# Leaving out the drain ahead of most vector and scalar instructions of a fused transformer layer

## The reference

```python
mod = (silu(c) @ wmod)                       # six vectors: sa, ca, ga, sb, cb, gb
ga, gb = sign(.) * maximum(abs(.), 0.25)     # each of the two gates
h = layernorm(x) * (1 + ca) + sa
q, k, v = split(h @ w_qkv)                   # 8 heads of 128
q_phi, k_phi = elu(q @ proj) + 1, elu(k @ proj) + 1        # 64 features
s = q_phi . k_phi over a window of 7 positions             # banded
x = x + ga * (normalised(s @ v) @ w_out + b_out)
h = layernorm(x) * (1 + cb) + sb
xn, se = rms_norm(h), rms_norm(slot_embeds)                # 4096 slots
logits = xn @ se.T
slots = softmax over positions(logits).T @ xn
processed = gelu(slots @ w1) @ w2                          # hidden 4096
out = x + gb * (softmax over slots(logits) @ processed)
```

## Time and profile before

| what | value |
|---|---|
| median of three runs | 4747.43 us |
| the three runs | 4679.46, 4799.58, 4747.43 us |
| the profiled execution | 4651.43 us |
| its span on the slowest core, from the first to the last instruction | 4649.3 us |
| spans of the eight cores | 4616.8 to 4649.3 us |
| busy time of TensorE's matmuls | 2645.6 us (57%) |
| busy time of VectorE | 1050.6 us (23%) |
| busy time of ScalarE | 688.5 us (15%) |

### The profile page before, as it was taken

How to read it: one execution, slowest core, us unless ns; L and a number is a source line. 1 busy time by engine, 2 the same in 40 slices (tenths; PEclk the granted TensorE clock), 3 DMA queues, 4 the chain that set the end, 5 groups by cost and what they waited for, 6 DMA issues and landing times. The chain is left out here.

```text
span 4649.3 us, 35458 instructions; the slowest of 8 cores (4616.8 to 4649.3 us)
## 1 busy us (share of the span) xinstructions
PE 2645.6 (57%) x11776; PEld 1229.4 (26%) x11776; DVE 1050.6 (23%) x2012; ACT 688.5 (15%) x1181; POOL 547.1 (12%) x1021
## 2 busy tenths in 40 slices
PE   4245344344333555555555558888599974554454
PEld 0222112111111222222222223333144432332222
DVE  1533222222554222222222200000301011111111
ACT  0101111111111111111111112222000001111111
POOL 4000000000000111111111125445200000000000
PEclk5567555565666777777777779999699986666667
DMA  8120111111111111111111151111622321111111
GB/s 119 50 48 19 23 23 23 36 32 41 55 55 41 34 34 34 34 34 37 41 37 34 32 104 62 62 59 62 124 73 73 87 63 55 54 63 55 54 55 59
DMA packets 138961, 241.91 MB, mean 52 GB/s; under 512 B 34967, under 2 KB 80279, under 8 KB 137758
## 3 DMA queue, kind: packets, MB, share of 16 engines
q0 software_dynamic: 78864, 138.49, 13.1%
q1 hardware_dynamic: 59918, 101.16, 7.2%
HBM read 201.85 MB, written 83.89 MB: 61 GB/s over the span
## 5 line engine op out<-in xcount | busy, mean ns | idle before, releaser
L1066 PE MATMUL pH<-slots_fm,w_bf 128*128 128x512 bf16 x2048 | 486.6, 401 | 117.6 <-DMA h_sp<-hbuf 73.4
L1153 PE MATMUL pP<-w_bf,hblk 128*128 128x512 bf16 x2048 | 458.3, 386 | 35.7 <-DVE w_bf L1131 20.6
L922 PE MATMUL pL<-xn_fm,sefs 128*128 128x512 bf16 x1024 | 282.3, 444 | 52.3 <-DVE sefs L913 52.3
L95 POOL DMA_DIRECT2D h_sp<-hbuf x512 | 271.9, 539 | 331.6 <-ACT hbuf L1077 320.9
L1066 PEld LDWEIGHTS pH<-slots_fm,w_bf 128*128 128x128 bf16 x2048 | 205.6, 102 | 398.2 <-issue 188.6
L994 PE MATMUL pDs<-xn_tm,atm 128*128 128x512 bf16 x1024 | 274.8, 436 | 31.6 <-DVE atm L986 31.6
L1153 PEld LDWEIGHTS pP<-w_bf,hblk 128*128 128x128 bf16 x2048 | 199.5, 98 | 295.6 <-issue 61.8
L1274 PE MATMUL pO<-proc_sm,w_smb 128*128 128x512 bf16 x1024 | 257.3, 419 | 15.8 <-DVE w_smb L1263 15.8
L95 POOL DMA_DIRECT2D L_sp<-lch x256 | 136.3, 541 | 1044.1 <-ACT lch L953 1005.7
L946 ACT ACTIVATE ach<-pL,colA,rscale_all 128x512 bf16<-128x512 f32 x128 | 99.5, 778 | 964.7 <-DVE colA L935 956.2
L977 PE MATMUL pAt<-ident_bf_s,ach 128*128 128x128 bf16 x512 | 64.8, 306 | 295.3 <-ACT ach L946 263.4
(11 more groups left out here) (185 smaller groups left out, 2481.2 us busy)
## 6 DMA issues: line engine op xcount, KB each, us to landing
L_sp<-lch POOLq DMA_DIRECT2D x256, 128.0 KB, 2.2
h_sp<-hbuf POOLq DMA_DIRECT2D x512, 64.0 KB, 1.8
lblk<-L_sp SPq DMA_DIRECT2D x8, 4096.0 KB, 16.7
se_st<-slot_embeds POOLq DMA_DIRECT2D x32, 512.0 KB, 3.6
wsl<-wmod POOLq DMA_DIRECT2D x96, 128.0 KB, 7.9
xst<-x SPq DMA_DIRECT2D x16, 512.0 KB, 3.3
xrs<-x SPq DMA_DIRECT2D x16, 512.0 KB, 3.8
x_sp<-x2b POOLq DMA_DIRECT2D x16, 512.0 KB, 4.5
```

The costliest lines, as they stand in the source:

```text
L95: self.ops[eng].append(lambda e: e.dma_start(dst, src).then_inc(h, 16))
L922: lmk = P.run("tensor", lambda e, buf=buf, j=j, nb=nb: e.matmul(pL[nb][:, 0:512], se_fs[buf][:, j * 128:(j + 1) * 128], xn_fm[:, j * N + n ...
L1066: e.matmul(pH[pbase + q][:, 0:512], w1_bf[:, j * HID + hc * 128:j * HID + (hc + 1) * 128], slots_fm[:, j * S + hf * 2048 + q * 512: j * S ...
L1153: e.matmul(pP[2 * (st % 2) + half][:, 0:512], h_blk[blk % 2][:, hc * HBW + st * 128: hc * HBW + (st + 1) * 128], w2_bf[:, hc * D + half * ...
```

## The change

`run` gets an argument `chain`, and the drain is put out only where it is true. A second method, `runf`, calls `run` without it. The calls at which the instruction does not read what the instruction right before it on the same engine has written become `runf`; the others stay. Of VectorE's 2012 drains 471 are left, of ScalarE's 950 there are 70 left: 1541 and 880 are gone, 2421 in all. No instruction is added, taken away or moved on any engine, and every semaphore wait stays where it was. The whole of the mechanism, and some of the 44 places at which it is used (the others are of the same form):

```diff
-    def run(self, eng, fn, sem=None, k=1):
-        if eng in ("vector", "scalar"):
+    def run(self, eng, fn, sem=None, k=1, chain=True):
+        if chain and eng in ("vector", "scalar"):
             self.ops[eng].append(lambda e: e.drain())
...
+    def runf(self, eng, fn, sem=None, k=1):
+        return self.run(eng, fn, sem, k, chain=False)
...
-                P.run("vector", lambda e, xs=xs, c=c: e.reduce_sum(
+                P.runf("vector", lambda e, xs=xs, c=c: e.reduce_sum(
                     colC[:, c:c + 1], xs[:], AX.X))
                 P.run("vector", lambda e, c=c: e.tensor_scalar(
                     colC[:, c:c + 1], colC[:, c:c + 1], 1.0 / D, None, ALU.mult))
...
                 for j in range(DJ):
-                    lastev = P.run("vector", lambda e, pt=pt, j=j, i=i: e.tensor_scalar(
+                    lastev = P.runf("vector", lambda e, pt=pt, j=j, i=i: e.tensor_scalar(
                         h1p[:, j * NP + 3 + i * 128: j * NP + 3 + i * 128 + 128],
...
                 for nb in range(4):
-                    P.run("vector", lambda e, nb=nb: e.reduce_max(
+                    P.runf("vector", lambda e, nb=nb: e.reduce_max(
                         colA[:, 8 + nb:9 + nb], pL[nb][:, 0:512], AX.X))
                 P.run("vector", lambda e: e.reduce_max(
                     colA[:, 12:13], colA[:, 8:12], AX.X))
...
-                    sfm_last = P.run("vector", lambda e, jj=jj, sc=sc: e.tensor_copy(
+                    sfm_last = P.runf("vector", lambda e, jj=jj, sc=sc: e.tensor_copy(
                         slots_fm[:, jj * S + sc * 128:jj * S + sc * 128 + 128],
...
                     for q in range(4):
-                        gel = P.run("scalar", lambda e, q=q, hc=hc, pbase=pbase:
-                                    e.activation(
+                        gel = P.runf("scalar", lambda e, q=q, hc=hc, pbase=pbase:
+                                     e.activation(
...
                 w2f_mk.append(P.run("vector", lambda e, hc=hc: e.tensor_tensor(
                     w2_bf[:, hc * D:(hc + 1) * D], w2_bf[:, hc * D:(hc + 1) * D],
-                    gb_rep[:], ALU.mult), "v"))
+                    gb_rep[:], ALU.mult), "v", chain=(hc == 0)))
```

More of the change, by code:

```diff
@@ L455, in build @@
                                 P.wait("vector", "v", m_vz)
-                            vev.append(P.run("vector",
-                                             lambda e, pv=pv, i=i, half=half, r=rows:
-                                             e.tensor_copy(
+                            vev.append(P.runf("vector",
+                                              lambda e, pv=pv, i=i, half=half, r=rows:
+                                              e.tensor_copy(
                                 v_tm[0:r, i * D + half * 512:i * D + half * 512 + 512],
@@ L535, in build @@
                         for b4 in (2 * h2, 2 * h2 + 1):
-                            P.run("vector", lambda e, b4=b4: e.tensor_scalar(
+                            P.runf("vector", lambda e, b4=b4: e.tensor_scalar(
                                 t_min_q[:, (b4 % 2) * 512:(b4 % 2) * 512 + 512],
                                 pp[4 + b4 % 2][0:64, 0:512], 0.0, None, ALU.min))
-                            P.run("vector", lambda e, b4=b4: e.tensor_scalar(
+                            P.runf("vector", lambda e, b4=b4: e.tensor_scalar(
                                 t_min_k[:, (b4 % 2) * 512:(b4 % 2) * 512 + 512],
                                 pp[b4 % 2][0:64, 0:512], 0.0, None, ALU.min))
-                        m_tmin = P.run("vector", lambda e: e.memset(colD[:, 1:2], 0.0), "v")
+                        m_tmin = P.runf("vector", lambda e: e.memset(colD[:, 1:2], 0.0), "v")
                         P.wait("scalar", "v", m_tmin)
-                        P.run("scalar", lambda e: e.activation(
+                        P.runf("scalar", lambda e: e.activation(
                             t_min_q[:], t_min_q[:], AF.Exp))
-                        m_exp = P.run("scalar", lambda e: e.activation(
+                        m_exp = P.runf("scalar", lambda e: e.activation(
                             t_min_k[:], t_min_k[:], AF.Exp), "s")
@@ L771, in build @@
                     for half in range(2):
-                        P.run("vector", lambda e, i=i, half=half: e.tensor_tensor(
+                        P.runf("vector", lambda e, i=i, half=half: e.tensor_tensor(
                             x2_b[i % 2][:, half * 512:(half + 1) * 512],
@@ L775, in build @@
                             x_rs[i % 2][:, half * 512:(half + 1) * 512], ALU.add))
-                    m_x2 = P.run("vector", lambda e: e.memset(colD[:, 2:3], 0.0), "v")
+                    m_x2 = P.runf("vector", lambda e: e.memset(colD[:, 2:3], 0.0), "v")
                     x2_mk.append(m_x2)
@@ L957, in build @@
                 P.wait("vector", "s", aemk[-1])
-                P.run("vector", lambda e: e.reduce_sum(
+                P.runf("vector", lambda e: e.reduce_sum(
                     colB[:, 12:13], colB[:, 8:12], AX.X))
@@ L1004, in build @@
                 for half in range(2):
-                    P.run("vector", lambda e, buf=buf, half=half: e.tensor_scalar(
+                    P.runf("vector", lambda e, buf=buf, half=half: e.tensor_scalar(
                         sl_sm[buf][:, half * 512:(half + 1) * 512],
                         pDs[half][:, 0:512], colB[:, 12:13], None, ALU.mult))
-                dis_last = P.run("vector", lambda e: e.memset(colD[:, 3:4], 0.0), "v")
+                dis_last = P.runf("vector", lambda e: e.memset(colD[:, 3:4], 0.0), "v")
                 P.wait("tensor", "v", dis_last)
@@ L1164, in build @@
                     for half in range(2):
-                        pev.append(P.run("vector",
-                                         lambda e, stt=stt, st=st, half=half:
-                                         e.tensor_copy(
+                        pev.append(P.runf("vector",
+                                          lambda e, stt=stt, st=st, half=half:
+                                          e.tensor_copy(
                             proc_sm[:, stt * D + half * 512:stt * D + half * 512 + 512],
@@ L1228, in build @@
                         for q in range(4):
-                            lt_ev = P.run("scalar", lambda e, stg=stg, q=q:
-                                          e.activation(
+                            lt_ev = P.runf("scalar", lambda e, stg=stg, q=q:
+                                           e.activation(
                                 l_tmb[:, stg * 2048 + q * 512:
@@ L1286, in build @@
                     for half in range(2):
-                        ol = P.run("vector",
-                                   lambda e, nt=nt, half=half: e.scalar_tensor_tensor(
+                        ol = P.runf("vector",
+                                    lambda e, nt=nt, half=half: e.scalar_tensor_tensor(
                             o_buf[nt % 2][:, half * 512:(half + 1) * 512],
```

56 lines of the change are left out of this document (28 added, 28 removed).

## The result

Ten runs of the changed kernel have a median of 4471.8 us (4394.96 to 4636.74), ten of the kernel before 4685.23 us (4653.77 to 4851.83). In some runs of either kernel the clock of a die is lowered for part of the time and the time is longer, and the comparison that follows is made without such runs. The ratio of the changed kernel to the one before is then 0.9458, with a 95% interval of 0.9402 to 0.9513: 5.4% faster, where 3.9% were forecast.

A forecast was written before the change was run, and what follows sets the result against it. Chains in which TensorE, VectorE and ScalarE wait for each other were taken as the bound. Gaps (165 us) plus drains behind waits (18 us) made 183 us, 3.9%, so 4561 us, range 4450 to 4680.

The forecast's parts named there:

- The stages and the chains: p0, heads, p1, p2, p5: engines wait in turn, so gaps count; p3 gains only at store waits; p4 gains 0.
- A gap on ScalarE: Between two independent ScalarE instructions, leaving out the drain saves 0.17 us.
- The pair of exponential and read: p2: the read of the running sum, without a drain, starts 0.10 us before its exponential ends; 0.18 us closer than drained.
- A gap on VectorE: Between VectorE instructions: 0.155 us saved for 512 columns, 0.12 for the small copies, 0.15 for line 370.
- half the fixed part: VectorE: overlap taken to hide half an instruction's fixed time, which is 0.16 us at 512 columns, 0.093 in the small copies.
- the roof: Upper bound, VectorE's whole fixed part hidden: 0.24 us a gap, 0.17 for 128-column copies; 285 us (6.1%) in all.
- the first rival: VectorE keeps its spacing, so only ScalarE and the waits gain: 85 us, 1.8%, 4661 us; chance 0.16.
- A drain behind a wait: Drain on an empty engine, 608 places in p0, heads, p1, p2, p5: 0.03 us each, 18 us.
- The comparison with TensorE's start: p2: one event releases TensorE and VectorE; drained VectorE starts 0.01 to 0.04 us later, taken as the drain's cost.
- the third rival: p2: TensorE's clock comes back, granted 0.77 to 0.85, 62 us more gained, about 4500 us; chance 0.09.
- The slower side: Clock taken away: p3 and p4 granted 0.66, not 0.945, 445 us longer, 5015 us in all; chance 0.04.
- I carry the ratio over: Whole kernel: the profiled execution's 183 of 4651.4 us applied to the 4747.4 us median, giving 4561 us.

The follow-up runs named there:

- p2_only: Kernel before with the drains left out in p2's loop alone: p2 gained 85 us (1133 us), no other stage moved by more than 2 us.
- waits_only: Kernel before without the changed kernel's dropped drains that stand right behind a semaphore wait; drains between instructions stay: ratio 0.9928, span -17 us.
- nop_instead: Changed kernel with a sequencer NOP in place of each of the 2421 drains left out: span 78 us longer than the changed kernel's.
- gaps_only: Changed kernel with the drain put back where an instruction stands right behind its own semaphore wait: span -185 us against the kernel before.

## Why the prediction was right or wrong

The forecast was 183 us of idle time of TensorE and nothing else. The stages' medians show 224 us less idle time and 40 less busy time (added up one by one they come to 1 us more than the 263 of the span). Three steps failed, two that made the gain too small and one that moved the range.

*The stages and the chains* were right. Every stage that was called a chain gained, p4 gained nothing, the transfers of the earlier trace rows that were called untouched stayed, and p3's was shorter by the gelus' part (73 to 56 us). p2_only shows that a stage's gain stays in the stage.

*A gap on ScalarE* (0.17) was right: 0.18 between exponentials, 0.19 between the small copies. The pair of exponential and read was a good proxy.

*A gap on VectorE* was undersized, and this is the first failed step: "half the fixed part". In the copies of 128 columns the whole of it is hidden: 0.167, where 0.12 was taken and 0.17 was the roof. For 512 columns the gap is 0.17, where 0.155 was taken; that is 0.095 of the fixed 0.16 us and not the whole. For line 370 the 0.15 was right. The Trainium skill's figure in "Vector Engine (DVE) Microarchitecture Reference", section "Measured stream behaviour on trn2", gave an estimated saving of 0.16 for 512 columns, and the trace agrees: the maxima start (2.48 - 0.68)/3 = 0.60 us apart, by that section an estimated 0.61. For the copies of 128 columns it would give an estimated 0.21 us from start to start, and the trace has 0.132. The rule of the Trainium skill behind the first rival ("VectorE: DVE Perf Modes", section "The DRAIN you can't avoid") does not hold here: with no drain instruction between, the next instruction starts 0.08 us before the end of the one before. Counted again with 0.17, the gaps make 184 us (by the prediction's own terms they are 1085, not 1087).

*A drain behind a wait* (0.03) was undersized too: 0.04 to 0.06 by the timelines and waits_only, 608 x 0.05 = 30 us. The comparison with TensorE's start could not show it, since TensorE's own start behind the same event was not a measure of VectorE's without a drain.

Both together make 214 us of idle time; the medians have 224.

*The clock* was put aside as two rivals, and this is the second failed step: the sum took TensorE's busy time as given. It fell by 40 us (p3 18, p5 11, p2 6, p1 3, and 2 in the rest). The mechanism of the third rival did occur, in that the transposes 908 kept the high clock in all but 3 chunks: 32.4 us in all before, 20.6 after, in the median of the cores. But it did not take p2's busy time down by 62: the first group of 32 matmuls went from 282 to 274 us and the second, 997, from 275 to 290, which leaves 6. p2's 668 us are the lowest of the eleven in the table, and next to them lie lengths of a chunk that cost 63 us more. That the change kept its whole gain in p2 is luck of this length; a version with four drains more a chunk showed 178 us in all. I had no way to see this in the trace of before. The slower side did not come: p3 and p4 were granted 0.93 and 0.94.

*The range in microseconds* failed by another step, the third: "I carry the ratio over". All terms were read from the profiled execution of 4651.4 us, and the ratio was then taken off 4747.4 us, the median of three runs that spread over 2.6%. Taken off 4651.4, the same sum gives 4468 us and the roof of 285 us gives 4366; the measured 4383 to 4444 us lie between them. The 263 us by which the spans shrank are less than that roof, so that the range was left is this step's doing, and that the gain came out 80 us larger than the sum is that of the other two. That the median of all ten runs (4471.8 us) lies in the range is luck and supports no term of the sum.

## What to carry to other kernels

A drain between two independent instructions costs 0.15 to 0.19 us on VectorE or ScalarE, at 128 columns as at 512, because it forbids their overlap; look for groups of short instructions that another engine waits for. This change kept the drain where an instruction reads what the one right ahead of it wrote, and no run here shows what happens without it there. Add up idle and busy time of TensorE apart: the first adds up over edits, the second jumps with the length of the loop, so that an edit of 20 us can show as 85, and a single timing of a part says little of that part. A wait for a transfer that appears once in every turn is worth a look at its queue first: two reordered loads brought as much (276 us) as 2421 drains.

## What the runs showed that I had not expected

- Without a drain VectorE starts eight PSUM copies of 128 columns every 0.132 us, so that a copy that lasts 0.215 us costs only its columns.
- A NOP in a drain's place is free between instructions and costs as much as the drain behind a wait (the stages of nop_instead and gaps_only agree within 4 us).
- On the same 3072 instructions of TensorE in p2, busy time ran from 668 to 731 us as the idle time ahead of one group changed by 0.7 us a chunk, and came back to 668.0 in a repeat; chunk by chunk, a group of the same 32 matmuls took 8.4 or about 10 us.
